# Update stage of a graph layer: residual as one multiply-add, sum written in place, second normalisation on ScalarE, deeper buffers and lags

## The reference, cut to what matters

```python
x0 = x
h  = layernorm(x0)                                  # first normalisation, mean and rstd per node
y  = silu(concat(h, agg) @ uW1 + ub1) @ uW2 + ub2
x1 = x0 + (h + y)                                   # the residual
t  = layernorm(x1)                                  # second normalisation
# then: 8 experts, top 2 of softmax(t @ router_w.T); out = x1 + t + weighted expert rows
```

## Time and profile before

| | |
|---|---|
| median of 3 runs | 3717.24 us (3708.7 to 3721.29) |
| the profiled execution | 3730.12 us, its span 3728.4 us |
| update stage in the profile | about 3009.4 to 3189.4 us |
| busy share of the whole span | TensorE 64%, VectorE 57%, ScalarE 43%, GpSimd 66% |

### The profile page before, as it was taken

One profiled execution on the slowest core, in us unless ns is written; L12 is line 12 of the kernel. 1 busy time (PEld: TensorE's weight loads), 2 busy tenths in 40 slices (PEclk: granted clock), 3 DMA queues, 4 the chain that ended last, 5 costly groups with the idle time before them and its releaser, 6 DMA issues. The chain is left out here.

```text
span 3728.4 us, 64620 instructions
## 1 busy us (share of the span) xinstructions
PE 2377.0 (64%) x13354; PEld 1924.0 (52%) x13355; DVE 2137.1 (57%) x6317; ACT 1601.5 (43%) x5331; POOL 2460.3 (66%) x2433
## 2 busy tenths in 40 slices
PE   0002770002888888888888878999999978107891
PEld 0001440001666666666666667777777767106781
DVE  7996760003555565656555566777777778432234
ACT  0000220002666566666666657777777744002330
POOL 0777777777888888888888866556666644483331
PEclk9999995556999999999999999999999999558996
DMA  5001330001222122222222232222222345333337
GB/s 114 2 2 16 66 67 2 2 2 39 52 52 54 49 54 51 51 52 53 51 51 53 52 51 67 63 61 63 62 62 63 62 140 155 106 85 101 103 99 220
DMA packets 175888, 237.82 MB, mean 64 GB/s; under 512 B 71575, under 2 KB 133889, under 8 KB 175323
## 3 DMA queue, kind: packets, MB, share of 16 engines
q0 software_dynamic: 85728, 144.80, 16.4%
q1 hardware_dynamic: 83082, 86.04, 8.1%
q10 hardware_dynamic: 7025, 6.40, 0.6%
HBM read 172.80 MB, written 63.30 MB: 63 GB/s over the span
## 5 line engine op out<-in xcount | busy, mean ns | idle before, releaser
L259 POOL DMA_INDIRECT edge_records<-stage x800 | 985.2, 1231 | 266.0 <-issue 224.0
L706 POOL DMA_INDIRECT work<-dst_half,stage_i x880 | 879.0, 999 | 248.0 <-issue 230.9
L936 PE MATMUL ps<-W2c,work 128*128 128x256 f32 x3520 | 874.3, 392 | 113.9 <-ACT work L874 73.3
L936 PEld LDWEIGHTS ps<-W2c,work 128*128 128x128 f32 x3520 | 643.7, 193 | 240.5 <-ACT work L874 103.9
L782 DVE TENSOR_TENSOR agg<-agg,ps 125x256 f32 x880 | 366.5, 416 | 548.9 <-remote 347.6
L945 PE MATMUL ps<-work 128*125 128x256 f32 x1760 | 468.1, 389 | 125.5 <-DVE agg L782 123.3
L861 ACT ACTIVATE work<-work 128x512 f32<-128x512 f32 x440 | 277.0, 630 | 486.0 <-DVE work L830 394.5
L945 PEld LDWEIGHTS ps<-work 128*125 128x125 f32 x1760 | 321.0, 189 | 212.9 <-issue 107.9
L830 DVE SCALAR_TENSOR_TENSOR work<-ps,work,b2c 128x256 f32<-128x256 f32 x880 | 382.1, 475 | 8.3 <-remote 5.3
L855 ACT ACTIVATE work<-ps 128x256 bf16<-128x256 bf16 x440 | 164.4, 374 | 508.7 <-PE ps L906 377.5
L714 POOL TENSOR_TENSOR work<-work 128x4 f32<-128x4 f32 (+1 forms) x221 | 231.1, 1046 | 225.7 <-DVE work L803 216.2
(11 more groups left out here) (208 smaller groups left out, 3343.4 us busy)
## 6 DMA issues: line engine op xcount, KB each, us to landing
work<-dst_half,stage_i POOLq DMA_INDIRECT x880
work<-routed_tokens SPq DMA_DIRECT2D x53, 257.0 KB, 2.7
routed_tokens<-work SPq DMA_DIRECT2D x26, 514.0 KB, 4.1
edge_records<-stage POOLq DMA_INDIRECT x800
work<-expert_rows SPq DMA_DIRECT2D x25, 320.0 KB, 5.9
update_node_half<-dpart SPq DMA_DIRECT2D x50, 125.0 KB
work<-update_node_half SPq DMA_DIRECT2D x25, 250.0 KB, 2.8
work<-expert_rows SPq DMA_DIRECT2D x25, 180.0 KB, 6.4
```

What stands on the lines that cost most here:

```text
L259: pool.indirect_dma_start(recd[h], bass.IndirectOffsetOnAxis(ap=stage[0:NB, i, c, 3:4].bitcast(i32), axis=0), stage[0:NB, i, c, :], None). ...
L706: pool.indirect_dma_start(bg[:, r, u, :], None, dstd, bass.IndirectOffsetOnAxis(ap=stage_i[:, c:c + 1], axis=0)).then_inc(gath[r], 16)
L936: last = t_.matmul(ps[:, 5 + s, u * D:(u + 1) * D], sT[:, a.mod(RT), u, k], W2c[:, k], start=(k == 0), stop=(k == KC - 1))
```

## The change

1. `xh` is made by VectorE in one multiply-add for each tile: xp * (1 + rstd) + ub2. The two coefficients 1 + rstd (`xscale`) and -mean * rstd (`xshift`) are made once at the start of the stage. GpSimd keeps only the power, which it writes straight into `mv3`.
2. x1 is made by one instruction for each tile, (product + xshift) + xh, and written straight into `agg`. ScalarE's copy (1191) is gone, and the statistics are taken from `agg`.
3. `mv3` now holds rstd and -mean * rstd; the second is one small VectorE instruction. The second normalisation is done by ScalarE as rstd * x1 + (-mean * rstd), with both factors read from a tensor. The routing stage uses the same two numbers in its own normalisation (multiply and add in place of subtract and multiply).
4. `xp` and `y1T` have four buffers in place of two. A load of `xp` waits for the `xh` of four pairs before it.
5. The lags are 1, 2, 4, 5, 6 in place of 1, 2, 3, 4, 5.
6. `padrow` lies in `rec`, the buffer of the edge records, in place of `work`.

```diff
-        xp = two(u=2)
-        hp = two(u=2)
+        RP = 4
+        xp = [cut(2 * D, "p (u n) -> p u n", u=2) for _ in range(RP)]
...
-        y1T = two("p (k n) -> p k n", KC * 2 * NB, k=KC)
+        y1T = [cut(KC * 2 * NB, "p (k n) -> p k n", k=KC) for _ in range(RP)]
...
-        UA, U1, U2, UT, UL = 1, 2, 3, 4, 5
+        UA, U1, U2, UT, UL = 1, 2, 4, 5, 6
...
-                        wait(sp, xh_ready, m.of(1, -1))
+                        wait(sp, xh_ready, m.of(1, 1 - RP))
...
-                        pool.wait_ge(hp_ready, b.of(1, 1))
-                        wait(pool, x1_kept, b.of(1, 1 - RH))
-                        wait(pool, tb_ready, b.of(1, 1 - RH))
-                        nc.gpsimd.tensor_tensor(xh[h][n_], xp[s][n_], hp[s][n_], ALU.add).then_inc(sx, 1)
-                        pool.wait_ge(sx, b.of(1, 1))
-                        nc.gpsimd.tensor_tensor(xh[h][n_], xh[h][n_],
-                                                ub2b[n_, :].unsqueeze(1).to_broadcast([NB, 2, D]), ALU.add).then_inc(xh_ready, 1)
...
-                        nc.gpsimd.tensor_tensor(rstd3[s][n_], var3[s][n_], half3[n_], ALU.pow).then_inc(rstd3_ready, 1)
+                        nc.gpsimd.tensor_tensor(mv3[n_, bass.ds(a.of(2), 2), 1], var3[a.mod(2)][n_], half3[n_], ALU.pow).then_inc(rstd3_ready, 1)
...
+                v.tensor_scalar(xscale[n_], mv1[n_, :, 1], 1.0, None, ALU.add).then_inc(xcoef, 1)
+                v.scalar_tensor_tensor(out=xshift[n_], in0=mv1[n_, :, 0], scalar=-1.0, in1=mv1[n_, :, 1],
+                                       op0=ALU.mult, op1=ALU.mult).then_inc(xcoef, 1)
...
-                        v.tensor_copy(mv3[n_, both, 0], pair3[r][n_, :, 0])
-                        v.tensor_copy(mv3[n_, both, 1], rstd3[r][n_])
-                        for u in range(2):
-                            last = v.tensor_scalar(tb[r][n_, u], xh[a.mod(RH)][n_, u], pair3[r][n_, u, 0:1],
-                                                   rstd3[r][n_, u:u + 1], ALU.subtract, ALU.mult)
-                        last.then_inc(tb_ready, 1)
+                        v.scalar_tensor_tensor(out=mv3[n_, both, 0], in0=pair3[a.mod(2)][n_, :, 0], scalar=-1.0,
+                                               in1=mv3[n_, both, 1], op0=ALU.mult, op1=ALU.mult).then_inc(mv3_ready, 1)
...
-                        v.tensor_tensor(xh[h][n_].rearrange("p u n -> p (u n)"), ps[n_, 4, :],
-                                        xh[h][n_].rearrange("p u n -> p (u n)"), ALU.add).then_inc(x1_ready, 1)
...
+                            last = v.scalar_tensor_tensor(out=agg[n_, t, :].rearrange("p t f -> p (t f)"),
+                                                          in0=ps[n_, 4, u * D:(u + 1) * D], scalar=xshift[n_, t],
+                                                          in1=xh[h][n_, u], op0=ALU.add, op1=ALU.add)
...
-                            last = v.tensor_scalar(hp[s][n_, u], xp[s][n_, u], mv1[n_, t, 0], mv1[n_, t, 1],
-                                                   ALU.subtract, ALU.mult)
-                        last.then_inc(hp_ready, 1)
+                            last = v.scalar_tensor_tensor(out=xh[m.mod(RH)][n_, u], in0=xp[s][n_, u], scalar=xscale[n_, t],
+                                                          in1=ub2b[n_, :], op0=ALU.mult, op1=ALU.add)
+                        last.then_inc(xh_ready, 1)
...
-                        nc.scalar.activation(agg[n_, bass.ds(a.of(2), 2), :], xh[a.mod(RH)][n_], ACT.Copy).then_inc(x1_kept, 1)
+                        act.wait_ge(mv3_ready, a.of(1, 1))
+                        wait(act, tb_tr, a.of(1, -1))
+                        for u in range(2):
+                            t = bass.ds(a.of(2, u), 1)
+                            last = nc.scalar.activation(tb[a.mod(2)][n_, u], agg[n_, t, :].rearrange("p t f -> p (t f)"), ACT.Identity,
+                                                        bias=mv3[n_, t, 0], scale=mv3[n_, t, 1])
+                        last.then_inc(tb_ready, 1)
...
-                                    mv3[n_, t, 0], mv3[n_, t, 1], ALU.subtract, ALU.mult).then_inc(ts_parts, 1)
+                                    mv3[n_, t, 1], mv3[n_, t, 0], ALU.mult, ALU.add).then_inc(ts_parts, 1)
```

More of the change, by code:

```diff
@@ L1005, in gnn_moe_kernel @@
         tT = two("p (k n) -> p k n", KC * 2 * NB, k=KC)
-        padrow = cut(XD * XW, "p (d w) -> p d w", d=XD)
+        padrow = rec[:, :, :].rearrange("p g f -> p (g f)")[:, 0:XD * XW].rearrange("p (d w) -> p d w", d=XD)
         raw3 = cut(12, "p (u s) -> p u s", u=2)
@@ L1009, in gnn_moe_kernel @@
         var3 = two("p u -> p u", 2)
-        rstd3 = two("p u -> p u", 2)
         half3 = cut(2)
@@ L1016, in gnn_moe_kernel @@
         fw_in = sem("fw_in")
-        xp_in = [sem("xp_in0"), sem("xp_in1")]
+        xp_in = [sem(f"xp_in{r}") for r in range(RP)]
         un_in = [sem("un_in0"), sem("un_in1")]
-        hp_ready = sem("hp_ready")
+        xcoef = sem("x_coefficients")
         xh_ready = sem("xh_ready")
@@ L1076, in step @@
                         empty_slots(m)
-                pipeline(sp, NP2, UA, 2, step, peel=2)
+                pipeline(sp, NP2, UA, RP, step, peel=2)
                 for g in range(NP2 * XD // 2, XT, XD // 2):
@@ L1161, in step @@
                     if m.within(NP2):
[L1162 to L1163 removed]
+                        dve.wait_ge(xp_in[s], m.per(RP, 32, 32))
                         for u in range(2):
                             t = bass.ds(m.of(2, u), 1)
[L1166 to L1168 removed]
+                            last = v.scalar_tensor_tensor(out=xh[m.mod(RH)][n_, u], in0=xp[s][n_, u], scalar=xscale[n_, t],
+                                                          in1=ub2b[n_, :], op0=ALU.mult, op1=ALU.add)
+                        last.then_inc(xh_ready, 1)
                 update(dve, step)
@@ L1187, in step @@
                                              ACT.Copy).then_inc(aggT_ready, 1)
-                    a = m - U2
+                    a = m - UT
                     if a.within(NP2):
-                        wait_apart(act, x1_ready, a.of(1, 1), passed_act)
-                        nc.scalar.activation(agg[n_, bass.ds(a.of(2), 2), :], xh[a.mod(RH)][n_], ACT.Copy).then_inc(x1_kept, 1)
+                        act.wait_ge(mv3_ready, a.of(1, 1))
+                        wait(act, tb_tr, a.of(1, -1))
+                        for u in range(2):
+                            t = bass.ds(a.of(2, u), 1)
+                            last = nc.scalar.activation(tb[a.mod(2)][n_, u], agg[n_, t, :].rearrange("p t f -> p (t f)"), ACT.Identity,
+                                                        bias=mv3[n_, t, 0], scale=mv3[n_, t, 1])
+                        last.then_inc(tb_ready, 1)
                     a = m - U1
@@ L1194, in step @@
                         act.wait_ge(y1b_ready, a.of(1, 1))
-                        wait(act, y2_ps, a.of(1, -1))
+                        wait(act, y2_ps, a.of(1, 1 - RP))
                         for k in range(KC):
-                            last = nc.scalar.activation(y1T[a.mod(2)][:, k], y1b[:, k], ACT.Silu, bias=ub1T[:, k:k + 1])
+                            last = nc.scalar.activation(y1T[a.mod(RP)][:, k], y1b[:, k], ACT.Silu, bias=ub1T[:, k:k + 1])
                         last.then_inc(y1_ready, 1)
@@ L1239, in step @@
                             for k in range(KC):
-                                last = t_.matmul(ps[n_, 4, u * D:(u + 1) * D], y1T[a.mod(2)][:, k, u * NB:(u + 1) * NB], uW2s[:, k],
+                                last = t_.matmul(ps[n_, 4, u * D:(u + 1) * D], y1T[a.mod(RP)][:, k, u * NB:(u + 1) * NB], uW2s[:, k],
                                                  start=(k == 0), stop=(k == KC - 1))
```

24 lines of the change are left out of this document (10 added, 14 removed).

## The result

The changed kernel takes 3679.99 us (median, 3675.33 to 3684.01), the kernel before 3713.88 us in runs beside it: a ratio of 0.9906, 95% interval 0.9888 to 0.9924. That is 33.9 us faster; 31 were forecast, and the time forecast was 3686 us.

The account below looks back on a forecast made before the run. VectorE, held up by GpSimd, then silu, then TensorE bound the update stage's step; afterwards TensorE would. 19 x (6.61 - 5.2) = 26.8 plus 5 at the start, rounded to 31: 3717.2 - 31 = 3686 us, range 3677 to 3702.

Parts of the forecast that it names:

- TensorE sets the step: Update stage: TensorE never waits, so its work sets each step at 5.2 us (5.21 summed) instead of 6.61; chance 0.80.
- VectorE's sum: Update stage: VectorE's work in a step adds up to 4.1 us, 4.4 at the upper bound, under TensorE's 5.21.
- GpSimd beside it: GpSimd's power, 0.80 us, beside VectorE's new first-normalisation pair: at worst the pair waits 0.8 us, VectorE 4.9 to 5.2.
- What frees VectorE: GpSimd's two additions hold up VectorE by about 1.1 us at L1134 and 0.9 at L1131; removing them ends this.
- Silu's 1.20 us covered by a step: TensorE's 1.20 us wait ahead of L1240 for silu L1197 is covered, since silu's result is used a whole step later.
- rival two: ScalarE reloads an activation table each step, two loads of 1.28 us: step 6.3 us, time 3709 us; chance 0.03.
- The rings: Dependency loops closing within two steps: product with uW2 through transposes 9.8 us, 4.9 a step; loads of x, 4.1 to 5.0.
- Transfers: Loads of x land in 2.8 us (2.5 to 4.5); their ring needs 4.1 to 5.0 us a step.
- Clock: TensorE, hardly ever idle, was expected to stay at full clock; before, it was 0.95 with four slow steps of 17.
- rival three: TensorE falls to half clock for long: step 9.4 us, 3770 us if for all 19 steps; chance 0.05.
- Start and end: First to fourth mark (additions L1156) 5 us shorter; end unchanged, 25.9 us behind the 23rd mark, set by weight transfers.
- Rival one: A ring or late load of x sets the step: 5.8 us a step, 17 us gain, 3700 us; chance 0.12.

Follow-up runs that it names:

- e5: Changed kernel plus two unused GpSimd additions per step behind the power: step 5.17 us, stage 150.1 us, no ratio (too few runs).
- e8: Changed kernel with xh made as before (VectorE pair, two GpSimd additions), new lags kept: step 5.05 us, stage 146.3 us, ratio 0.9918.
- e2: Changed kernel with the old lags 1, 2, 3, 4, 5 (arithmetic alone): step 6.01 us, stage 168.6 us, ratio 0.9964.
- e1: Kernel before with only the new lags, four `y1T` buffers and `padrow` in `rec`: step 5.01 us, stage 145.6 us, ratio 0.9898.
- e9: Kernel before with the new lags, GpSimd's first addition written into `hp` so it needn't wait for `tb`: step 5.44 us, stage 154.6 us, ratio 0.9901.
- e10: Kernel before, old lags, GpSimd's first addition made to wait for the same step's `tb`: step 5.59 us, stage 160.4 us, ratio 0.9936.
- e6: Changed kernel with half the inner dimension of the uW1 and router products left out: step 4.73 us, stage 138.6 us, ratio 0.9922.

## Why the prediction was right, point by point

- **TensorE sets the step: right, 5.07 us against 5.2.** The sum was 5.21, the trace has 1.73 + 1.69 + 0.79 + 0.89 = 5.10. The term that was off is the first: I took 1.83 us from a product that began after a wait, 1.99 busy; without one it is 1.89 busy and 1.73 to the next. The 19 steps gave 29.1 us where 26.8 were forecast, 2.3 us more.
- **VectorE's sum: on the safe side.** 3.56 us against 4.1. Both multiply-add pairs take 0.88 (0.95 allowed).
- **GpSimd beside it: neither case cost anything.** The power took 0.73 us beside the pair, which stayed at 0.88; at the stage's end, with no pair beside it, the power takes 0.70. So the exclusion of these two, which the prediction priced at up to 0.8 us, doesn't show. In e5 and e8 two SBUF inputs did contend with GpSimd's additions, on the small instruction.
- **What frees VectorE: right in what holds it, but not the only thing that releases it.** The prediction put the saving on VectorE down to the two additions that go. In this change they do go, and e2, with the old lags, has the same 3.56 us. But e1 keeps them and has the whole gain, because the lags move them through the four buffers `xh`. The prediction missed that, and its number couldn't show it: that came out right with either release, since TensorE sets the step. Each half of the change removes the collision by itself; only the lags also cover silu. Hence e1 equals the whole, and e2 gives a third of it.
- **Silu's 1.20 us covered by a step: right.** It needed the collision gone too: e9 has the cover with half of the collision, and not the whole gain (5.44 us), e10 the reverse (5.59).
- **ScalarE: right.** 1.09 us for the pair of `tb` (1.1), no table load: rival two is dead. The Trainium skill's "ScalarE: Activation LUTs" ("Table sets: the hidden batching unit") had said so, and the trace agrees: Identity, Copy and silu alternate in the trace of the step above with no load between them.
- **The rings: right in order, 0.2 us off.** 4.7 a step by e6, under TensorE's 5.1.
- **Transfers: right, but closer than forecast.** The loads of x land in 2.9 us (median, 5.5 at worst: 2.8 and 4.5). VectorE waited for one twice in the 19 steps, 1.5 us in all, and TensorE never for it.
- **Clock: right.** 1.00 over the 19 steps. The reading of before was off by one: of the 17 steps of the earlier trace rows three are slow, and the fourth begins where that window ends, so it is four of 19. The share that decides rival three doesn't hang on it.
- **Start and end.** 6.2 us against 5, and -0.3 against 0.

Together 29.1 + 6.2 - 0.3 = 35.0 where I summed 31.8. The 3.2 us are the step (2.3) and the start (1.2), less the end (0.3). The forecast of 3686 us was off by 6: these 3 of the saving, and 3 because the kernel before took 3713.88 us in the runs beside the change and not the 3717.2 that I had started from. Rival one (a load or a ring sets the step) did not happen; by e6 the ring over `tb` closes 0.3 us below TensorE's step, and the ring over the loads of x isn't longer, since VectorE waited for x only once in e6's 19 steps.

## What to carry to other kernels

When a lag or a number of buffers is changed, follow every wait that runs through the buffers, on the idle engines too. In e1 a longer lag delayed GpSimd's additions by one wait and so took 1.7 us a step off VectorE's busy time, with no instruction changed. If two engines get in each other's way, first try one wait that holds the engine with time to spare: it gave two thirds of the step's gain here (e10). And before work is taken off an engine, ask whether the ring through the step closes any sooner; e2 took 2.3 us a step off VectorE's busy time, and its step fell by 0.6.

## What the hardware showed

- GpSimd's additions held some of VectorE's instructions until they ended, however small these were: a copy of 2 elements for 1.0 to 1.2 us (0.17 alone), a multiply-add on 2 elements with two SBUF inputs for 0.8 to 1.2 (0.16), a pair of subtract and multiply on 125x256 for 1.8 (0.73). Others ran beside them at their usual length: the multiply-add pair with an input in PSUM (0.88, e5), and the statistics, which have one input in SBUF (0.75, e1).
- The four slow steps of TensorE in the 19 before came behind gaps of 1.16 to 1.20 us (clock 0.95 over the stretch), but other products behind gaps of 1.16 to 1.21 us kept their 1.99 us, as in the earlier trace rows. E2 has gaps of about 0.65 us (0.8 at most) and e10 of about 0.3 (0.4 at most), and both show a clock of 1.00 over all 19 steps. What decides between a slow and a full-speed step, these runs don't tell.
- Transfers at 252 GB/s, a share of 0.87, beside the same loop left its step at 5.08 us, with loads of x in it.
